# A post-norm decoder layer on one core: cell sums with the gated tile held on TensorE, new orders on all engines, and other places for the unread products

## The reference, cut to what matters

```python
x = layernorm(x + attn(x))          # 16 sequences of 128 tokens, width 128, 16 heads of 8
x = layernorm(x + xattn(x, ctx))    # below
x = layernorm(x + ffn(x))           # one linear layer, x and weight rounded to blocks of 6-bit floats

# attn: q and k pass a linear layer, a 3-tap convolution and a joint projection;
scores = einsum('bhqd,bhkd->bhqk', Q, K) / sqrt(DK) * tau[..., None] + delta[:, :, None, :]
out = linear(einsum('bhqk,bhkd->bhqd', softmax(scores), V), out_w, out_b)

# xattn: an mLSTM cell with 4 heads of 32; queries are x, keys and values the context
D = exp(log_D - max_log_D)                      # decay of the forget and input gates, causal
C = einsum('bhsd,bhtd->bhst', qh, kh) / sqrt(dh) * D
normalizer = maximum(abs(C.sum(-1, keepdims=True)), exp(-max_log_D))
hst = einsum('bhst,bhtd->bhsd', C / (normalizer + eps), vh)
hn = (hst - mean(hst)) / sqrt(var(hst) + 1e-5) * scale
```

## Time and profile before

| | |
|---|---|
| median of 3 runs (lowest to highest) | 213.35 us (212.99 to 213.43) |
| profiled execution, its own time | 213.28 us |
| its span, first to last instruction | 211.3 us |
| mean granted TensorE clock | 0.966 |
| PE busy, matmuls | 193.3 us (91%), 2103 records |
| PE weight loads | 122.0 us (58%) |
| DVE busy | 159.6 us (76%), 432 instructions |
| ACT busy | 140.8 us (67%), 427 instructions |
| POOL busy | 102.4 us (48%), 218 instructions |

### The profile page before, as it was taken

How to read it: one execution, slowest core, us unless ns; L and a number is a source line. 1 busy time by engine, 2 the same in 40 slices (tenths; PEclk the granted TensorE clock), 3 DMA queues, 4 the chain that set the end, 5 groups by cost and what they waited for, 6 DMA issues and landing times. The chain is left out here.

```text
span 211.3 us, 6086 instructions
## 1 busy us (share of the span) xinstructions
PE 193.3 (91%) x2103; PEld 122.0 (58%) x2103; DVE 159.6 (76%) x432; ACT 140.8 (67%) x427; POOL 102.4 (48%) x218
## 2 busy tenths in 40 slices
...
PEclk9965599999999999999999999999999999999999
...
DMA packets 12137, 9.38 MB, mean 44 GB/s; under 512 B 2796, under 2 KB 10828, under 8 KB 12108
## 3 DMA queue, kind: packets, MB, share of 16 engines
...
...
## 5 line engine op out<-in xcount | busy, mean ns | idle before, releaser
L1129 DVE TENSOR_REDUCE nm<-score 128x8 f32<-128x1024 f32 x32 | 38.8, 1218 | 6.9 <-PE score L662 6.8
L520 ACT ACTIVATE prob<-score 128x1024 f32<-128x1024 f32 x32 | 32.5, 1020 | 11.1 <-PE score L674 11.0
L662 PE MATMUL score<-km,qf 32*128 32x512 f32 x128 | 33.9, 637 | 1.2 <-DVE nm L1129 0.3
L668 PE MATMUL score<-qm,kf 32*128 32x512 f32 x128 | 33.8, 636 | 0.0
L388 POOL CAST nmx<-nm 128x16 bf16<-128x16 f32 x16 | 5.5, 341 | 31.2 <-issue 26.2
L674 PEld LDWEIGHTS score<-nmT,sel 32*128 32x128 bf16 x256 | 10.1, 93 | 16.2 <-issue 16.2
L359 POOL TENSOR_SCALAR u<-xTp,dw 128x512 f32<-128x512 f32 x16 | 13.7, 868 | 10.3 <-PE score L740 5.4
L883 PE MATMUL bankPV<-prob,vw 128*32 128x128 f32 x512 | 17.2, 275 | 0.0
L583 ACT ACTIVATE dec<-dec,g 128x128 f32<-128x128 f32 x56 | 17.1, 393 | 0.0
L656 PE MATMUL bankP<-xTp,wT 128*128 128x512 f32 x36 | 16.8, 602 | 0.0
L422 POOL TENSOR_TENSOR hsl<-hs,rows 128x256 f32<-128x256 f32 (+1 forms) x9 | 6.0, 672 | 20.4 <-ACT hs L599 20.4
(11 more groups left out here) (264 smaller groups left out, 491.1 us busy)
## 6 DMA issues: line engine op xcount, KB each, us to landing
...
```

Source lines behind the costliest of these rows:

```text
L520: nc.scalar.activation(prob[:, i % 2, k:k + 2, :].rearrange("p k s -> p (k s)"), sc[:, 512 * k:512 * (k + 2)], ACT.Exp, scale=SQ_SCALE).th ...
L662: ins = mm(sc[:, 512 * k:512 * (k + 1)], qf[r, n, :], km[r, n % (2 * CB)].rearrange("p j s -> p (j s)"), start=True, stop=True)
L668: mm(sc[:, 512 * k:512 * (k + 1)], kf[r, n, :], qm[r, n % (2 * CB)].rearrange("p j s -> p (j s)"), start=True, stop=False)
L1129: nc.vector.tensor_reduce(nm[:, i % 3, J * k:J * (k + 2)], sc[:, 512 * k:512 * (k + 2)].rearrange("p (h s) -> p h s", s=S), AX_X, ALU.max, ...
```

## The change

1. **Cell sums.** `hst` now holds `cc` (128 x 128) and streams `ctm`, which has 33 columns a head (`CW = DH + 1`), the last being 1. The sums of a head come out in the right orientation with the row sum as column 33, 8 products in a full group. The `onew` products, `hE`, `hT` and their tiles are gone. `hs` copies the bank (264 columns in a full group) and releases it; `ha`, now a step of its own, takes the absolute row sums from `hs` in SBUF, and `na` waits for it. `cm` writes one sequence at a time, since `ctm` has gaps now.
2. **Orders.** All five lists are written anew. DVE, POOL and SP have the same steps as before in another order; ACT has nine `ha` in place of nine `hE`; PE has no `hT`.
3. **Unread products.** `light` writes to score bank S3 in place of PV, and stands among the folded weights too: 23 products for 12. `fill` has 46 for 56; four stand directly behind `aT.8` and `ffn.4`. Together 69 for 68.

```diff
+CW = DH + 1
...
-        cT = sb("cT", [P, B, S]); ctm = sb("ctm", [P, B, NH, DH]); hTs = sb("hTs", [P, 2, 3 * S]); onew = sb("onew", [P, 64]); gc = sb("gc", [P, B, GW])
+        cT = sb("cT", [P, B, S]); ctm = sb("ctm", [P, B, NH, CW]); gc = sb("gc", [P, B, GW])
...
                 elif name == "cm":
                     b0, nb = GR[i]
                     act.wait_ge(cm_ps, i + 1)
-                    nc.scalar.activation(ctm[:, b0:b0 + nb].rearrange("p v h d -> p v (h d)"),
-                                         pb[:, 0:YW * nb].rearrange("p (v c) -> p v c", v=nb)[:, :, 0:D], ACT.Copy).then_inc(cm_sb, 1)
+                    if i == 0:
+                        act.wait_ge(zeroed, 1)
+                    for v in range(nb):
+                        ins = nc.scalar.activation(ctm[:, b0 + v, :, 0:DH],
+                                                   pb[:, YW * v:YW * v + D].rearrange("p (h d) -> p h d", d=DH), ACT.Copy)
+                    ins.then_inc(cm_sb, 1)
...
-                elif name == "hE":
-                    w = S * (GR[i][1] + 1)
+                elif name == "hs":
+                    w = NH * GR[i][1]
                     act.wait_ge(hst_ps, i + 1)
                     if i >= 2:
-                        act.wait_ge(hT_ps, i - 1)
-                    nc.scalar.activation(hTs[:, i % 2, 0:w], yb[:, 0:w], ACT.Copy).then_inc(hE_done, 1)
-                elif name == "hs":
-                    nb = GR[i][1]
-                    act.wait_ge(hT_ps, i + 1)
-                    if i >= 2:
                         act.wait_ge(hl_done, i - 1)
+                    nc.scalar.activation(hs[:, i % 2, 0:w].rearrange("p h d -> p (h d)"), yb[:, 0:w * CW], ACT.Copy).then_inc(hs_done, 1)
+                elif name == "ha":
+                    w = NH * GR[i][1]
+                    act.wait_ge(hs_done, i + 1)
+                    if i >= 2:
                         act.wait_ge(na_done, i - 1)
-                    nc.scalar.activation(ha[:, i % 2, 0:NH * nb].rearrange("p (h v) -> p h v", v=nb),
-                                         yb[:, S * nb:S * (nb + 1)].rearrange("p (h x) -> p h x", h=NH)[:, :, 0:nb], ACT.Abs)
-                    nc.scalar.activation(hs[:, i % 2, 0:nb].rearrange("p v c -> p (v c)"), yb[:, 0:S * nb], ACT.Copy).then_inc(hs_done, 1)
+                    nc.scalar.activation(ha[:, i % 2, 0:w], hs[:, i % 2, 0:w, DH], ACT.Abs).then_inc(ha_done, 1)
...
                     free("Y")
-                    if i == 0:
-                        pe.wait_ge(zeroed, 1)
                     for v in range(nb):
                         for h in range(NH):
+                            o = CW * (nb * h + v)
                             k = nb * h + v
-                            mm(yb[DH * h:DH * (h + 1), S * v:S * (v + 1)], ctm[:, b0 + v, h, :], cc[:, i % 2, S * k:S * (k + 1)], start=True, stop=True)
-                    for v in range(nb):
-                        for h in range(NH):
-                            k = nb * h + v
-                            ins = mm(yb[DH * h:DH * (h + 1), S * nb:S * (nb + 1)], onew[:, 32 - v:64 - v], cc[:, i % 2, S * k:S * (k + 1)],
-                                     start=(v == 0), stop=(v == nb - 1))
+                            ins = mm(yb[:, o:o + CW], cc[:, i % 2, S * k:S * (k + 1)], ctm[:, b0 + v, h, :], start=True, stop=True)
                     ins.then_inc(hst_ps, 1)
...
-                        mm(pvb[:], fil[:], fil[:].unsqueeze(1).to_broadcast([P, NH, S]), start=True, stop=True)
+                        mm(sc[:, 1536:2048], fil[:], fil[:].unsqueeze(1).to_broadcast([P, NH, S]), start=True, stop=True)
...
 PE_ORDER = """
-    light.8 tx.0 light.1 ab.0 light.3 mT.0 tx.1 hw.0 mT.1 wT.0 tx.2 wT.1 cT.0 del.0 tau.0 K.0 Q.0 gw.0 tx.3 K.1 cg.0 aa.0 fill.2 tau.1 fill.2 cT.1 fill.1
+    light.8 tx.0 light.1 ab.0 light.4 mT.0 tx.1 mT.1 light.1 hw.0 light.3 wT.0 light.4 cT.0 wT.1 light.2 K.0 tau.0 Q.0 del.0 tx.2 gw.0 tau.1 tx.3 cT.1
```

More of the change, by code:

```diff
@@ L60 @@
[L60 to L63, removed]
@@ L64 @@
-    ld.8 hT.7 dT.5 fill.2 ffn.5 fill.5 hst.8 hT.8 dT.6 fill.2 ffn.6 fill.8 dT.7 fill.2 ffn.7 fill.9 dT.8 fill.2 ffn.8
+    light.8 tx.0 light.1 ab.0 light.4 mT.0 tx.1 mT.1 light.1 hw.0 light.3 wT.0 light.4 cT.0 wT.1 light.2 K.0 tau.0 Q.0 del.0 tx.2 gw.0 tau.1 tx.3 cT.1
+    cg.0 aa.0 K.1 ow.0 aa.1 edT.0 Q.1 nmT.0 rc.0 fill.2 v1.2 V.0 nmT.1 fill.2 v2.2 V.1 fill.2 del.1 pv.0 cm.0 v1.3 K.2 v2.3 nmT.2 cm.1 pv.1 v1.4 edT.1
+    pT.0 V.2 v2.4 aT.0 nmT.3 y1.0 v1.5 nmT.4 pv.2 yT.0 v2.5 gF.0 del.2 pv.3 v1.6 tau.2 MT.0 pT.1 del.3 aT.1 nmT.5 tau.3 y1.1 Q.2 v2.6 Q.3 qk.0 edT.2
@@ L65 @@
+    gF.6 aT.7 hst.5 MT.5 pv.15 y1.7 MT.6 qk.6 yT.7 pT.8 dT.4 aT.8 ffn.4 fill.4 gF.7 y1.8 fill.2 MT.7 ld.7 qk.7 yT.8 hst.6 fill.2 dT.5 hst.7 gF.8 ffn.5
+    fill.1 MT.8 qk.8 ld.8 fill.8 hst.8 dT.6 fill.2 ffn.6 fill.12 dT.7 fill.4 ffn.7 fill.3 dT.8 fill.2 ffn.8
 """
 DVE_ORDER = """
-    fil.0 cent.0 sel.0 ab.0 tapT.0 tapD.0 mT.0 tapT.1 hw.0 mT.1 tapD.1 wT.0 tapD.2 wd.0 bias.0 wT.1 tapT.2 kf.0 bias.1 tapT.3 qf.0 gw.0 qs.0 tapD.3 kf.1
-    mX.0 mY.0 tapT.4 mY.1 mX.1 tapD.4 mX.2 qf.1 cg.0 qs.1 mX.3 ow.0 vz.0 mY.2 vz.1 tapD.5 mY.3 tapT.5 tapD.6 kf.2 mX.4 rc.0 vz.2 mY.4 dr.0 att.0 gc.0
@@ L70 @@
[L70 to L73, removed]
@@ L78 @@
[L78 to L79 removed]
+    fil.0 cent.0 sel.0 ab.0 tapT.0 tapD.0 mT.0 tapT.1 mT.1 hw.0 tapT.2 wT.0 wd.0 wT.1 tapT.3 bias.0 tapD.1 bias.1 kf.0 tapD.2 qf.0 gw.0 qs.0 tapD.3 cg.0
+    mY.0 mX.0 kf.1 tapD.4 mX.1 ow.0 mY.1 rc.0 qf.1 mX.2 vz.0 tapT.4 vz.1 mY.2 tapD.5 gc.0 mX.3 tapD.6 kf.2 mY.3 qs.1 gc.1 tapD.7 mX.4 dr.0 vz.2 att.0 mY.4
@@ L89 @@
[L89 to L91 removed]
+    xT.0 geD.0 xT.1 cT.0 geT.0 geT.1 thT.0 geD.1 geT.2 geT.3 thD.0 xT.2 thT.1 xT.3 geD.2 cT.1 geD.3 exp.0 edx.0 edc.0 nmT.0 eY.0 nmT.1 eX.0 gelu.1 thD.1
```

72 lines of the change are left out of this document (35 added, 37 removed).

## The result

The changed kernel takes 209.12 us (median of 4 runs, 206.43 to 212.61) where the kernel before takes 213.28 on the same chip: ratio 0.9756, 95% interval 0.9721 to 0.9791, faster. The profiled execution took 209.32 us for a span of 207.3.

A forecast was written before the change was run, and what follows sets the result against it. It took DVE to bound the start, TensorE's queue 45 to 165 us, and nearly full ACT and DVE 165 to 195. Sum: 213.3 - 4.6 + 1.9 + 0.9 - 4.0 = 207.5 us, range 203.5 to 212.5.

The forecast's parts named there:

- the forecast case: Whole kernel: the main case of 207.5 us, own range 205 to 209.7, chance 0.46.
- start: Up to the first maximum: K.0 earlier, clock held by added products, DVE deciding; -4.6 us, ends -5.3 and -1.5.
- middle: TensorE's stage up to the last scores: +1.9 us for five groups' cell sums, +0.9 for steps moved ahead.
- tail: From sequence 15's first exponential to the end: ACT work moved ahead, round trip gone; -4.0 us, ends 0 and -4.9.
- kf.0: Sign at the start, on DVE: this step would start near 26.5 us, where it started at 28.78.
- the first maximum: Sign at the start, on DVE: it would come near 32.5 us instead of 37.59; at 36 the prediction is wrong.
- the end of the last scores: Sign at the end of TensorE's stage: near 167.3 us for 169.1; 169 or later would be wrong.
- The second rival: Start: added products do not hold the clock, which returns at 26; qf.0 gains 1.5 us, total 210.6; chance 0.16.
- Rival 4: Clock not held and tail not shortened, with a somewhat larger cell-sum term: 213.3 us, no change; chance 0.05.
- the first rival: Cell sums: weight loads do not overlap the stream, 0.44 us a product, total 219; chance 0.11 with a milder form.
- qk.5 and dT.3: TensorE steps of 0.7 and 0.3 us moved ahead of the last scores, priced at +0.9 us.
- The fills behind aT.8 and later are cover: Tail, on TensorE: the unread products there were called cover, with 68 unread products becoming 69 in all.

The follow-up runs named there:

- experiment 8: Changed kernel with the four fills ahead of gF.7 replaced by seven unread products that do not wait for aT.8's copy: 212.1 us, ratio 0.987.
- experiments 5: Kernel before with only the orders changed, keeping its old cell sums with copy and transposes back: 219.93 us, ratio 1.0304.
- 6: Changed kernel's orders with the old cell sums, hs two steps behind hE in groups 0 to 4: 220.47 us, ratio 1.0322.
- experiments 3: Kernel before with only the cell sums changed, orders otherwise as before: 221.59 us, ratio 1.037.
- 4: Kernel before with the new cell sums in the old orders, plus thirteen more unread products in the tail: 216.62 us, ratio 1.0153.
- experiment 9: Changed kernel with five more unread products at the start, ahead of the head weights' products: 211.53 us, ratio 0.991.
- 12: Changed kernel with seven non-waiting unread products for the four fills ahead of gF.7, and more fills behind y1.8: 209.34 us, ratio 0.9777.

## Why the prediction was right, and where not

**The total.** 207.5 forecast, 209.12 measured, in the forecast case's own range of 205 to 209.7. Against the profiled execution: start -3.8 (for -4.6), middle +2.6 (for +2.8), tail -2.8 (for -4.0), which sums to -4.0, the difference of the spans. The forecast gains at the start and in the tail were both too large; of the 5.8 us in all, 4.2 came. Of its signs kf.0 came as said (26.41 for 26.5), the first maximum at 33.92 for 32.5 and the end of the last scores at 167.96 for 167.3.

**The start.** DVE decided, as argued, but the size was off by 0.8: gw.0's copies wait 0.99 us for TensorE, which the sum left out. Runs whose clock stayed at 1.00 reach the other end: v1.2 at 39.58, 5.3 us early. The second rival's price was wrong in the step "with 1.00 back at 26, Q.0 ends near 31.5": without the added products the clock was back at 23.4, K.0 ended at 24.3, and qf.0 came 4.5 us early (28.65), not 1.5. K.0 ahead of tau.0 and del.0 did the work; the added products were worth 0.3 us of the profiled start, and up to 1.8 (41.42 to 39.58) where the clock stays at 1.00, if no kernel without them gets that. Rival 4's 213.3 does not follow either: its parts give 213.3 - 1.5 + 1.9 + 0.9 = 214.6, before any larger term of the cell sums.

**The cell sums.** The price of 0.23 us a product stands, and the first rival with its 0.44 is out. By the rows the surcharge is 1.84 - 1.4, 0.44 us a group and 2.2 for five, where the sum put 1.9; with qk.5 and dT.3 the middle would have been +3.1 for the measured +2.6. Why do 33 columns cost nearly as much as y1's 136? Three products that hold 128 x 128 and stream a single column, at a clock of 1.00 in experiment 8's run, are 0.20 us apart:

```profile
13.75 0.72 PE L726 MATMUL bankT<-cols,mT 128*128 128x1 f32 x6
14.34 0.36 PE L727 MATMUL bankT<-cols,abT 128*128 128x1 f32 x2
```

So most of the 0.23 is there without the stream, and the two loads a product, 192 ns each by their records and busy for 15.1 of the products' 15.5 us, are the likely pace. y1's stream alone would need some 0.23 us, an estimate from K.0's six records of 512 columns, 2.6 us in the changed kernel (21.41 to 23.99). If its loads came on top of that, a y1 product would take over 0.4 us; it takes 0.24, so there loads and stream overlap. With 33 columns the stream is too short to tell. The Trainium skill ("TensorE: Matmul & The Clock Gate", Part 3, The mechanism) says that a load is pulled ahead of running products for another row group or for a background weight buffer, and also that it overlaps them only when the row groups differ. y1's products share all rows, so the trace disagrees with the second statement and not with the first.

**The tail.** The order's gain is real: from the last scores to y1s.8 it is 11.8 to 14.3 us in the runs with the new orders (16.1 with doubled products) and 15.3 to 15.7 in those with the old, whichever the form of the sums. What failed is the step "The fills behind aT.8 and later are cover": they stood ahead of gF.7 and y1.8 for 1.7 us at 1.2 GHz. Taking them away did not pay, since the clock fell later instead (experiment 8).

**What the sum did not have.** It added the parts as if they were independent. Alone, the new cell sums cost 8 us (my terms: some 1), 3.0 between v1.2 and the last scores and 6.0 behind y1s.8. The new orders alone cost 6 to 7 us (my terms: 5 to 6 faster than before); together they save 4.2. Two ties make the difference. From a group's last product to its sums in SBUF it was 2.1 to 4.6 us in groups 0 to 4 before (round trip and queues) and is 0.4 now (1.2 in group 4); the new DVE order needs them sooner than a round trip allows (experiments 5, 6). And with the new products in the old order TensorE's clock is down in the tail (experiments 3, 4). The new order escapes the long fall in most of its runs; that its fills and products fall otherwise is a likely reason, but no run isolates it. That the sum of my terms came out near is in part luck, as it knew of neither tie.

**Open.** What decides in a given run whether the clock falls at 14 us, or in the tail, was not found: experiment 9 did not prevent the one, nor 8 and 12 the other.
